# Gated linear attention: products of keys and values on four diagonal tiles of the array instead of one quarter of rows

## The reference

```python
B, L, DIM, H, D = (4, 128, 128, 8, 32)
dict(x=..., W_in=..., b_in=..., W_qkva=..., b_qkva=..., W_y=..., b_y=..., W_out=..., b_out=...,
     h0_re=jax.random.normal(ks[5], (H, D, D), jnp.float32),
     h0_im=jax.random.normal(ks[6], (H, D, D), jnp.float32))
```

```python
gain[h, j] = sum over the 32 tokens s of block j:  K[s, h, :].T @ V[s, h, :]     # 32 x 64 (real | imaginary)
```

## Time and profile before

| | us |
|---|---|
| median of 3 runs | 4078.03 |
| lowest, highest | 4077.9, 4082.77 |
| the profiled execution's own time | 4057.76 |
| its span | 4056.0 |
| TensorE matmuls busy in the span | 3493.4 |
| TensorE weight loads busy in the span | 2208.0 |
| VectorE busy | 2420.1 |
| ScalarE busy | 1594.6 |

### The profile page before, as it was taken

The page is one execution under the profiler, slowest core; times in us unless marked ns, Lnnn a source line. Parts: engine busy times, 40 slices in busy tenths (PEclk is TensorE's granted clock), DMA queues, the critical chain, the costliest instruction groups (busy, mean ns, idle before and its releaser), DMA issues. The chain is left out here.

```text
span 4056.0 us, 124079 instructions
## 1 busy us (share of the span) xinstructions
PE 3493.4 (86%) x55256; PEld 2208.0 (54%) x55256; DVE 2420.1 (60%) x6248; ACT 1594.6 (39%) x2941; POOL 537.9 (13%) x564
## 2 busy tenths in 40 slices
PE   3877777679999999999987796999999999999985
PEld 1326665225555555555556442566666666666672
DVE  3757776337776666777675112566666666666545
ACT  1653333355443344444321243444444344444323
POOL 1212222000000000000000000222222222222210
PEclk9996667788888889889765697999999999999967
DMA  2000000121111111111000001000000000000000
GB/s 88 0 0 1 1 1 1 43 72 47 51 31 44 34 44 39 39 45 39 13 3 3 17 0 44 2 3 3 3 2 3 3 3 2 3 3 3 2 3 23
DMA packets 37029, 77.11 MB, mean 19 GB/s; under 512 B 7696, under 2 KB 11152, under 8 KB 35472
## 3 DMA queue, kind: packets, MB, share of 16 engines
q1 hardware_dynamic: 36496, 69.17, 5.3%
HBM read 64.83 MB, written 4.33 MB: 17 GB/s over the span
## 5 line engine op out<-in xcount | busy, mean ns | idle before, releaser
L1366 PE MATMUL ps<-g_hs,g_fc 128*128 128x512 f32 x448 | 282.5, 716 | 38.3 <-ACT g_hidden L1488 21.1
L1488 ACT ACTIVATE g_hidden<-ps 128x512 f32<-128x512 f32 x224 | 133.3, 595 | 391.4 <-PE ps L1366 390.8
L2133 PE MATMUL ps<-d_hp,d_w_k 128*128 128x512 f32 x512 | 281.1, 635 | 0.0
L1257 PEld LDWEIGHTS ps<-g_Q,g_K 32*32 32x32 f32 x12288 | 193.1, 113 | 142.7 <-issue 55.0
L2211 POOL TENSOR_TENSOR d_sq<-d_QK 128x512 f32<-128x512 f32 x128 | 133.1, 1040 | 930.0 <-ACT d_QK L2262 768.7
L1380 PE MATMUL ps<-g_hidden,g_proj 128*128 128x512 f32 x448 | 251.4, 656 | 0.0
L1257 PE MATMUL ps<-g_Q,g_K 32*32 32x32 f32 (+1 forms) x12288 | 223.9, 217 | 31.0 <-DVE g_H L1526 10.0
L2231 ACT ACTIVATE d_F<-ps 128x128 f32<-128x128 f32 x256 | 70.8, 276 | 345.4 <-PE ps L2042 342.2
L1225 POOL COPY g_xb<-X 128x512 f32<-128x512 f32 x8 | 7.3, 907 | 1242.6 <-DVE X L1686 1131.5
L1366 PEld LDWEIGHTS ps<-g_hs,g_fc 128*128 128x128 f32 x448 | 81.7, 214 | 150.2 <-ACT g_hidden L1488 79.5
L2406 DVE SCALAR_TENSOR_TENSOR d_conv<-ps,w_conv_q,d_conv 128x511 f32<-128x511 f32 (+2 forms) x192 | 142.3, 741 | 34.8 <-ACT d_conv L2256 30.9
(11 more groups left out here) (479 smaller groups left out, 7885.3 us busy)
## 6 DMA issues: line engine op xcount, KB each, us to landing
g_hs<-gate_rows SPq DMA_DIRECT2D x56, 256.0 KB, 3.5
g_fc<-in_c_fc_dram SPq DMA_DIRECT2D x56, 256.0 KB, 3.9
g_proj<-in_c_proj_dram SPq DMA_DIRECT2D x56, 256.0 KB, 2.8
X<-in_x_dram SPq DMA_DIRECT2D x1, 2048.0 KB, 10.8
w_c_fc<-in_c_fc_dram SPq DMA_DIRECT2D x1, 2048.0 KB, 7.9
w_c_proj<-in_c_proj_dram SPq DMA_DIRECT2D x1, 2048.0 KB, 12.3
ex_root<-gate_rows SPq DMA_DIRECT2D x1, 2048.0 KB, 14.7
h_rows<-k SPq DMA_DIRECT2D x1, 2048.0 KB, 6.3
```

Of the source, the lines that this page charges most:

```text
L1257: ins = e.matmul(later(scored, n_), keys_, queries(n_, planes, r_, 4 * i + j), start=(turn_ == 0 and part == 0 and n_ != 1), stop=(part == 1),
L1366: e.matmul(P[2], fc[:, n % 2, ts(f, C)], hs[:, n % 2], start=True, stop=True).then_inc(pe.steps, pe.did(now(f"u{i}")))
L1488: e.activation(r[:, slot], P[2], ACT.Relu).then_inc(act.steps, act.did(now(f"r{i}")))
L2133: ins = e.matmul(b, w_k[:, j, ts(H, C)], hp_of(u)[:, j:j + T], start=(j == 0), stop=(j == TAPS - 1))
```

## The change

In gains the outer loop was over the block j, so a turn took one quarter of rows (block j) with all four quarters of columns (heads). Now the outer loop is over turn_, and inside it j runs over all four blocks, each with head (turn_ + j) % 4. A turn then takes four tiles of which no two share a quarter of rows or a quarter of columns. Over the four turns every pair of block and head comes once, as before. Where a result goes in PSUM, its two parts and their order, the number of turns, the waits and the semaphores stay. In a turn before, the four results went to the same 64 columns of bank P[1] in four quarters of partitions; now they go to four different runs of 64 columns, again in four quarters of partitions. No other engine's instructions are touched, and TensorE's sequence of lines, shapes and waits is the same; only operand slices and tile positions of line 1273 differ.

```diff
                         e.wait_ge(pe.steps, pe.at(now(f"s{i}3")))
-                        for j in range(4):
-                            if j:
+                        for turn_ in range(4):
+                            if turn_:
                                 ins.then_inc(pe.steps, pe.did())
                                 e.wait_ge(pe.steps, pe.n)
-                            rows = ts(j, 32)
-                            for part, h4 in ((part, h4) for part in range(2) for h4 in range(4)):
+                            for part, j in ((part, j) for part in range(2) for j in range(4)):
+                                rows, h4 = ts(j, 32), (turn_ + j) % 4
                                 ins = e.matmul(P[1][ts(h4, 32), 256 + j * 64:320 + j * 64], KT[rows, (KR, KI)[part], i, ts(h4, 32)],
                                                V[rows, i, 4 * c["sg"] + h4, (slice(32, 96), slice(0, 64))[part]], start=(part == 0), stop=(part == 1),
                                                tile_position=(32 * j, 32 * h4))
```

## The result

| | us |
|---|---|
| the changed kernel, median of 6 runs | 4058.29 |
| lowest, highest | 4049.17, 4060.69 |
| the kernel before, median of 6 runs | 4077.97 |
| lowest, highest | 4067.78, 4084.76 |
| ratio, with its 95% interval | 0.9947 (0.9929 to 0.9965) |

The account below looks back on a forecast made before the run. The prediction took TensorE's own sequence to bound the stage from 942 to 2253 us. Its one term, 256 turns x 0, left the median of 4078 us unchanged (chance 0.83), with a range of 4069 to 4087 us.

Parts of the forecast that it names:

- Pace of a turn: Gains, line 1273: 16 records on four diagonal tiles keep 0.43 us a turn; 256 turns x 0 = 0.
- line 2042 against line 2085: Delta rule: 32 records on four diagonal tiles, one bank, take 0.45 us; 8 on one tile take 0.43.
- The waits: Line 1273 between turns of gains: three waits a call stay, near 54 us over the stage.
- One bank, four quarters of rows: Rival in gains: row quarters writing P[1] are served one at a time, 232 us slower, 4310 us; chance 0.05.
- Loads that hide only now: Rival in gains: weight loads overlap matmuls only across row quarters, 6.4 us faster, 4072 us; chance 0.04.
- The cost of the change is then the answer to one question: Gains: only whether 16 records run at another pace on four row quarters than on one matters; answered with 0.
- that rival: Better clock over the stage: fewer falls to the half level behind gains, 49 us saved, 4029 us; chance 0.05.
- The price of the rival: Better clock: 157 us less at the half level x 0.31, from gains calls of 1.97 against 2.86 us, 49 us.
- The bounds of the sum: Gains, 256 turns: at most 6.4 us saved by a shorter first step, or 3 us lost between turns and calls.

Follow-up runs that it names:

- the bench: Two kernels without layers, gains-like calls in several tile layouts with fillers; at 128 columns of filler, mean clock 0.52 on one quarter of rows, 1.00 on four.
- column: Layout in a kernel without layers: a turn on four quarters of rows, one of columns, four banks; mean clock 1.00 with fillers of 128, 256 and 384 columns.
- the diagonal: The changed kernel's layout in a kernel without layers: four quarters of rows and four of columns, one bank; mean clock 1.00 with a filler of 128 columns.
- gains and scores: The changed kernel with the scores (line 1257) also laid out on four quarters of rows a turn: 4045.35 us, 0.9905 of the kernel before.
- the threefold turns: Each turn's eight products of gains issued three times: 4318.94 us on top of the kernel before, 4192.12 us on top of the changed kernel.

## Why the prediction was wrong

- **Pace of a turn: right.** The step that took line 2042 against line 2085 for the pace of a diagonal holds: 0.43 us and 1.97 us a call as before, and equal blocks in the bench.
- **The waits: right.** Line 1273 waits on itself at 0.25 us a turn as before, 53.5 us in all against 53.8.
- **One bank, four quarters of rows: right to reject.** No turn got longer, in the kernel or in the bench; column with four banks and the diagonal with one are equal.
- **Loads that hide only now: right to reject.** The slices with eight loads beside four matmuls look the same in both kernels.
- **"The cost of the change is then the answer to one question": this step failed.** It took the granted clock as given, and so put the clock's term at nothing. The layout leaves each turn's time alone and changes how long the clock stays at its half level: 474 us of the stage before, 430 after. That was the whole effect as far as the runs show. The prediction had it as a rival with a chance of 0.05 and 4029 us.
- **The argument against that rival was weak.** It rested on one stretch, 1621.5 to 1625.0, with products on two and on four quarters of rows after which the clock fell all the same. Those were products with 32 moving columns on tiles of 32x64. The bench shows what such turns are worth: on four quarters of rows they still had 0.51 with 384 columns of filler, where the turns of gains, with 64 moving columns on tiles of 32x32, had 1.00 with 128. The row could not speak for gains, and no row of the trace of before could: its 64-column products on small tiles were on one quarter of rows (gains) or on two (a third of the scores' records), never on four. I should have kept a chance for it as for an unknown, and a range that reached it.
- **The price of the rival: about right per microsecond, too large in amount.** The loss of 0.31 us for each us at the half level came from calls of gains alone, and the half-level stretches that I showed hold products of 128x512 instead. Two of those records take 1.12 us at the full level and 2.08 at the half, which is a loss of 0.46 us for each us:

```profile
1607.46 1.12 PE L1366 MATMUL ps<-g_hs,g_fc 128*128 128x512 f32 x2
...
1064.48 2.08 PE L1366 MATMUL ps<-g_hs,g_fc 128*128 128x512 f32 x2
```

Over whole stages the loss came out at 0.28 to 0.40, so the 0.31 was near by luck as much as by reasoning. The amount was wrong: a third of 472 us was assumed, 157 us, and 44 went. The clocks of all runs say much the same. The changed kernel's clock is 0.869 on average; in the 34 runs of before it is 0.860. A difference of 0.009 is 2 x 0.009 x 4070 = 73 us less at the half level, worth 23 us at 0.31 each, where the medians differ by 20. The clock alone is enough to explain the gain.
- **The bounds of the sum.** The 6.4 us of the lower bound use 0.025 us a turn, where the rows cited show 0.08 - 0.06 = 0.02, so 5 us; nothing hangs on it.

Why so little of the half-level time went, though the bench holds 1.00 throughout, was read from the kernel but not tested apart: gains is some 2 us of each quarter of a batch, and scores and outputs around it still ran on two quarters of rows. The step from gains alone to gains and scores, and the threefold turns, point the same way.

## What to carry to other kernels

When small products are tiled on the array, compare layouts by the quarters of rows that work at the same time, not by the number of tiles alone: at an equal clock four tiles cost the same on one quarter of rows or on four, but in this stage the clock spent less time at its half level with four. A change that leaves every instruction's time at a given clock alone can still move the total, so the clock belongs into the sum as a term of its own wherever the trace shows both levels. And one execution against one execution can't show half a per cent here: the single runs of the kernel before in one job spread from 4061.53 to 4092.65 us.

## What the runs showed of the hardware

- Turns of eight f32 products of 32x32 by 64 columns, with waits and a filler of 128 columns: mean granted clock 0.52 on one quarter of rows, 0.52 on two, 1.00 on four. With 512 columns of filler: 0.52, 1.00, 1.00. With 640 and more: 1.00 in all three.
- Four tiles of different quarters of rows and one quarter of columns, into four banks, hold the clock like the diagonal (1.00), and eight products one after another on one tile don't (0.50 with 512 columns of filler, with TensorE busy for 98% of the time).
- Four quarters of rows may write one bank side by side, each into its own quarter of partitions, without a loss of time: 0.43 us for the 16 records of a turn either way.
- Where products of 32x32 tiles alternate with products of 32x64 tiles, a group of 16 loads comes every 0.36 us at the full level, though it lasts 0.26 to 0.32 us.
- In this stage a microsecond at the half level cost 0.28 to 0.40 us of time; for a pair of 128x512 records alone it is 0.46, for a call of gains 0.31.
